# A convolution, a gate and two feed-forward layers on one core: how x reaches its phase layout, and where the context vector is added

## The chip, the cores and the metric

One core of one Trainium2 chip. The metric is the device time of one execution in microseconds (us), the median of the runs. Engines are named as the profile names them: PE (matrix products), PEld (its weight loads), DVE (vector engine), ACT (scalar engine), POOL (GpSimd), SP (the queue that issues most DMAs). A name with a q behind it (SPq, ACTq) is that engine's instruction queue, issuing DMAs.

## What is computed

x has 128 samples of 32 channels by 512 positions, all float32. Only the first layer matters here:

```python
out = conv1d(x, weight, taps=9, pad=4, groups=4)          # per sample, 32 -> 32 channels
ctx = einsum('nd,od->no', cond, c_weight)                  # (128, 32)
h   = out + ctx[:, :, None] + bias[None, :, None]          # a token = (sample, channel), 512 features
logits = h @ W_gate + b_gate                               # 8 experts, top 2 of them
y   = mean over the 2 chosen e of relu(h @ W_e[e] + b_e[e])
x   = x + y
```

There are 4,096 tokens, so 8,192 (token, expert) pairs. The second layer (a per-sample 32 by 32 mix of channels, then one 512 by 512 product with weights unpacked from 4 bits) is the same in both kernels.

## The kernel before

The work runs in three stages. **Stage 1** goes over 32 groups of 4 samples (128 tokens each): it makes the convolution, the gate's logits and the token rows, and scatters each token row to the lists of its two experts in DRAM. **Stage 2** goes over 71 blocks of 128 list entries and multiplies each by its expert's weights. **Stage 3** adds the two results of each token to x and computes the second layer. PE does the stages one after the other; the first block of stage 2 is `product(0, 0)`.

The five engines each run an instruction list of their own, in order, written out by hand as `step1(g, j)` per engine; semaphores carry the dependences. The loop over groups is a hardware loop of four groups a turn for groups 4 to 15, and unrolled elsewhere. What matters in stage 1 is how x becomes the stationary operand of the convolution. A tile `phases` holds, on partition 32*q + i, the positions 4*l + q of input channel i, for l = 0..127 and each of the 4 samples of the group. So three products per sample (`SHIFTS`) make the whole convolution, 12 in a group (L1169).

Per group the kernel before does the following.

- SP loads x of a group, 256 KB, to 128 partitions of `xt`, a ring of four slots (L403), each load when the slot's reader is done. After every four groups it queues a 1 MB load of one expert's weights (`load_we`) and a 257 KB write of zeros (`zero_head`). Once in four groups it also loads 256 KB of `ctx_bc`, the context of those groups' tokens repeated on all partitions (L400), from a copy of it in DRAM (`ctx_d`).
- DVE transposes x in 32 by 32 blocks while it gathers every fourth position (`transpose_x`, L694), two groups ahead. PE transposes four 128 by 128 pieces of that to PSUM (`transpose_phases`, L1098). ACT copies them to `phases` (L567). `phases` and `ring_a` have two slots.
- PE makes the convolution (L1169). DVE adds the context while it evicts (`hT`, L807). PE multiplies each 128 columns of `hT` by the gate's weights beside an identity (L1157, `gate_and_rows`), which gives four partial logits and the token rows; DVE sums the partials (`partial`, L816) and adds `bg_bc` (L825); ACT copies the token rows out, in two copies (`tok`, L584), and two key columns (L574). Then DVE finds the two experts, ending in `chosen` (L854), PE counts ranks with them (L1143, L1144), and POOL scatters (L524).

The order on each engine in step g: PE: convolution of g, transposes for g+1, ranks of g-2, gate of g-1. The gate of g-1 waits for `hT` of g-1, `partial` of g-2 and the `tok` copies of g-2. DVE: `hT` of g, transposition for g+2, then the small instructions for g-1 and g-2. ACT: phase copy for g+1, keys of g-2, token rows of g-1. ACT further issues the loads of the experts' biases in steps 18 to 21, and in steps 24, 25 and 27 does three activations of the second layer's small network (L600, L603, L606), two of them with a table load.

At the end of stage 1 the `xt` slots are reused for lists read back from DRAM: SP's `list_step` loads list a (four DMAs of 64 KB, each to 32 partitions, L434, and one of keys, L437), and for the first four lists waits for `xT_ready` of group 28 + a (L428). DVE transposes list 0 (L921) between its steps 29 and 30, list 1 between 30 and 31 (L943 to L946).

At the start, SP loads the condition and its weights, then the convolution's weights (four small DMAs, L374), then four groups of x. DVE and ACT pick the taps out of them (`pick_taps`, L363), six copies each of 32 by 128 whose reads step 60 bytes; PE transposes them. Eight dummy transposes (`warm_up`) stand ahead of the tap transposes and eight more ahead of the first convolution.

## Time and profile before

| | us |
|---|---|
| median of 3 runs (range) | 514.61 (514.56 to 514.78) |
| the profiled execution's own time | 515.17 |
| its span, first to last instruction | 513.4 |
| stage 1, from the first convolution to the first `product` | 11.6 to 149.7 |
| stage 2, to about | 390 |
| stage 3, to the end | 513 |

| DMA traffic of stage 1, KB a group (from the page's sizes) | |
|---|---|
| x in | 256 |
| expert weights, 1024 KB every fourth group | 256 |
| zeros, 257 KB every fourth group | 64 |
| context, 256 KB every fourth group | 64 |
| scattered rows, 2 times 257 KB | 514 |

Two readings of the page need care. PE's busy share is high in all stages, but they have different limits, so an edit is priced in its own stage. And the modelled length of a matmul overlaps the next one; for PE it is the distance from one start to the next that counts.

### The profile page before, as it was taken

To read this page: it belongs to the slowest core of one execution; us is meant where nothing else is said; L and a number is where in the kernel's file an instruction comes from. 1 tells how busy PE (TensorE), PEld (TensorE's weight loads), DVE (VectorE), ACT (ScalarE), POOL (GpSimd) and SP (SyncE) were. 2 spreads that over 40 slices of the span, in tenths; PEclk is the share of its full clock that TensorE was granted. 3 is DMA by queue.
4 is the path that set the end of the run, shared out by engine and by line. 5 is a ranking of instruction groups with operands and counts; after the bars stand their busy time and mean duration, and the time that the engine had idled before them with its cause. 6 is when DMAs were issued, how large, how long until landed. Compare 5 with 4: busy or idle time off the path is not lost. (4 is left out here: it accounts for less than half of the span.)

```text
span 513.4 us, 10342 instructions
## 1 busy us (share of the span) xinstructions
PE 496.1 (97%) x2412; PEld 329.5 (64%) x2413; DVE 347.0 (68%) x1082; ACT 121.0 (24%) x277; POOL 153.3 (30%) x178
## 2 busy tenths in 40 slices
PE   6999999999999999999999999999997999999996
PEld 5999999999964444444444444444544676767674
DVE  4588888888866547573354445444445899999996
ACT  3232333334421111111111111111123222222220
POOL 9144444444447322233323323332224000000000
PEclk9999999999998999999999999999999999999999
DMA  4969978999885686676665767675554798888852
GB/s 111 290 216 291 274 270 287 324 364 324 235 220 165 200 229 156 166 203 172 176 176 162 184 163 200 163 188 158 150 147 141 252 343 278 288 284 281 296 180 102
DMA packets 91442, 113.07 MB, mean 220 GB/s; under 512 B 25438, under 2 KB 62222, under 8 KB 90372
## 3 DMA queue, kind: packets, MB, share of 16 engines
q1 hardware_dynamic: 73200, 71.26, 49.3%
q0 software_dynamic: 11664, 36.24, 19.3%
q10 hardware_dynamic: 6536, 5.10, 3.5%
q8 instruction: 16, 0.26, 0.2%
q14 instruction: 26, 0.21, 0.1%
HBM read 67.55 MB, written 46.52 MB: 222 GB/s over the span
## 5 line engine op out<-in xcount | busy, mean ns | idle before, releaser
L1196 PE MATMUL bank<-we,lT 128*128 x536 | 233.6, 597 | 1.7 <-DVE ring_a L935 1.6
L1196 PEld LDWEIGHTS bank<-we,lT 128*128 128x128 f32 x536 | 101.7, 191 | 129.0 <-issue 128.8
L935 DVE TENSOR_TENSOR ring_a<-bank,be_bc 128x512 f32<-128x512 f32 x71 | 48.9, 690 | 104.4 <-PE bank L1196 50.4
L541 POOL DMA_INDIRECT pairs_d<-ring_b,pair_i x71 | 71.1, 1002 | 161.3 <-DVE pair_i L924 113.7
L1169 PE MATMUL bank<-wconv,phases 128*128 128x128 f32 x768 | 91.8, 276 | 0.7 <-ACT phases L567 0.7
L620 ACT ACTIVATE ring_b<-ring_a 128x512 f32<-128x512 f32 x71 | 44.7, 631 | 196.7 <-DVE ring_a L935 181.5
L1169 PEld LDWEIGHTS bank<-wconv,phases 128*128 128x128 f32 x768 | 89.1, 193 | 0.9 <-ACT phases L567 0.9
L524 POOL DMA_INDIRECT lists_d<-token_list,row_i x64 | 62.9, 983 | 83.6 <-DVE row_i L845 50.1
L921 DVE STREAM_TRANSPOSE lT<-xt 128x512 f32<-128x512 f32 x71 | 49.8, 702 | 5.7 <-DMA keys<-lists_d 5.4
L1263 PE MATMUL bank<-wq,high 128*128 128x512 f32 x128 | 37.4, 414 | 3.4 <-PEq L1211 3.4
L1157 PE MATMUL bank<-wg,lT 128*128 128x136 f32 x256 | 37.4, 289 | 1.1 <-DVE partial L816 1.1
L694 DVE STREAM_TRANSPOSE ring_a<-xt 128x512 f32<-128x512 f32 x32 | 35.3, 1102 | 0.0
L1267 PE MATMUL bank<-wq,low 128*128 128x512 f32 x128 | 34.5, 391 | 0.0
L567 ACT COPY phases<-bank 128x512 f32<-128x512 f32 x32 | 19.2, 600 | 64.5 <-PE bank L1098 49.2
L807 DVE TENSOR_TENSOR lT<-bank,rows_r 128x512 f32<-128x512 f32 x32 | 22.1, 690 | 16.3 <-PE bank L1169 13.1
L1157 PEld LDWEIGHTS bank<-wg,lT 128*128 128x128 f32 x256 | 31.8, 190 | 1.3 <-issue 1.2
L1242 PE MATMUL bank<-mix_bd,we 128*128 128x128 f32 x224 | 32.2, 287 | 0.0
L1242 PEld LDWEIGHTS bank<-mix_bd,we 128*128 128x128 f32 x224 | 27.3, 191 | 5.7 <-DVE we L1048 5.6
L584 ACT COPY token_list<-bank 128x256 f32<-128x256 f32 x64 | 20.7, 376 | 31.0 <-issue 17.1
L1267 PEld LDWEIGHTS bank<-wq,low 128*128 128x128 f32 x128 | 24.0, 188 | 5.5
L675 ACT CAST high<-bank 128x512 fp32r<-128x512 f32 x32 | 18.7, 586 | 36.3 <-PE bank L1242 36.3
L1263 PEld LDWEIGHTS bank<-wq,high 128*128 128x128 f32 x128 | 21.8, 190 | 7.0 <-issue 4.2
(194 smaller groups left out, 401.4 us busy)
## 6 DMA issues: line engine op xcount, KB each, us to landing
xt<-lists_d SPq DMA_DIRECT2D x284, 64.0 KB
xt<-in_x SPq DMA_DIRECT2D x60, 256.0 KB, 4.1
we<-pairs_d SPq DMA_DIRECT2D x28, 512.0 KB, 4.8
we<-in_L_ffn_W_e SPq DMA_DIRECT2D x8, 1024.0 KB
out<-orow_list SPq DMA_DIRECT2D x32, 256.0 KB, 2.8
lists_d<-orow_list SPq DMA_DIRECT2D x8, 257.0 KB
be_bc<-in_L_ffn_b_e ACTq DMA_DIRECT2D x4, 512.0 KB
words<-pairs_d POOLq DMA_DIRECT2D x4, 512.0 KB, 5.4
```

The source lines that it names most:

```text
L524: pool.indirect_dma_start(lists_d, bass.IndirectOffsetOnAxis(ap=row_i[:, j, k:k + 1], axis=0), token_list[:, j, :], None, bounds_check=E * ...
L541: pool.indirect_dma_start(pairs_d, bass.IndirectOffsetOnAxis(ap=pair_i[:, s % DR:s % DR + 1], axis=0), ring_b[:, s % U, :], None, bounds_c ...
L620: act.activation(ring_b[:, j, :], ring_a[:, j % 2, :], ACT.Relu, scale=0.5).then_inc(result_ready, 1)
L694: dve.transpose(ring_a[:, ja % 2, :].rearrange("m (h q i) -> m q h i", h=MH, q=PH), xt[:, ja, :].rearrange("c (h l q) -> c q h l", h=MH, q ...
L921: dve.transpose(lT[:, ja, :].rearrange("m (p h r) -> m h p r", p=PH, h=MH), xt[:, ja, :].rearrange("r (h p l) -> r h p l", h=MH, p=PH)).th ...
L935: dve.tensor_tensor(ring_a[:, j % 2, :], ps_exp[j % 2][:, :], be_bc[:, bass.ds(expert, 1), :].rearrange("p a n -> p (a n)"), ALU.add).then ...
L1157: mm = pe.matmul(ps_both[:, p // 2, cols], hT[:, ja % 2, p * P:(p + 1) * P], wg[:, p, :], start=True, stop=True)
L1169: mm = pe.matmul(ps_conv[j % 2][:, s * P:(s + 1) * P], phases[:, j % 2, s, t:t + P], wconv[:, t, :, :].rearrange("k p o -> k (p o)"), star ...
L1196: mm = pe.matmul(ps_exp[j % 2][:, :], lT[:, j, p * P:(p + 1) * P], we[:, bass.ds(expert, 1), p, :].rearrange("m a n -> m (a n)"), start=(p ...
L1242: mm = pe.matmul(ps_mix[a % 2][:, q * P:(q + 1) * P], y_of(a)[:, q * P:(q + 1) * P], mix_bd[:, a, :], start=True, stop=True)
L1263: pe.matmul(ps_lin[j][:, :], high[:, j % 2, q * P:(q + 1) * P], wq[:, q, :], start=(q == 0), stop=False, skip_group_check=True)
L1267: mm = pe.matmul(ps_lin[j][:, :], low[:, j % 2, q * P:(q + 1) * P], wq[:, q, :], start=False, stop=(q == PH - 1), skip_group_check=True)
```

## The change

x is loaded so that partition 32*j + c of `xt` (j the ring slot) holds channel c of all four samples, 32 partitions a load (`x_quad`, `x_sub`). `phases` is then filled by four copies of 32 partitions by 512 elements, whose reads step 16 bytes and whose output lies on another quadrant of 32 partitions (`split_phase`): phase 0 by DVE, phases 1 to 3 by ACT. DVE's gathering transposition, PE's four transposes and ACT's copy from PSUM go, with `ps_ph`. Both engines now split two groups ahead, when the convolution of g is done.

The context is no longer added to `hT`. `ctx_col` holds, per partition (sample, channel) and group, context plus `fside`. ACT adds it as a bias in the two row copies (Identity activations), and the logits get it as `gate_bias` = context times the column sums of the gate's weights, plus `b_gate`; both tables are made once, in step 0. The copy of the context in DRAM and its loads go. At the start the first x and the convolution's weights are loaded first, the latter half by SP and half by ACT, and one of the two `warm_up` calls goes. SP's first four list loads now wait for both splits of all 32 groups.

```diff
+        x_sub = x.rearrange("(g s) c l -> g c s l", s=SUB)
         out_g = out.rearrange("(g s) c l -> g (s c) l", s=SUB)
...
         cw_sb = sb("cw_sb", [C, P])
-        cwT = sb("cwT", [P, C])
...
+        def split_phase(copy, q, jq, jb):
+            return copy(phases[q * C:(q + 1) * C, jb, :, 1:P + 1],
+                        x_quad[jq].rearrange("c s (l q) -> c q s l", q=PH)[:, q, :, :])
...
+            sp.dma_start(x_quad[0], x_sub[0]).then_inc(x_in[0], 16)
+            sp.wait_ge(wfull_zero, 1)
+            for s in range(2):
+                rows = slice(s * CG, (s + 1) * CG)
+                sp.dma_start(wfull[rows, rows, PH - 1:PH - 1 + TAPS], conv_w[rows]).then_inc(convw_in, 16)
             sp.dma_start(cond_sb[:, :], cond).then_inc(cond_in, 16)
             sp.dma_start(cw_sb[:, :], ctx_w).then_inc(cond_in, 16)
-            sp.wait_ge(wfull_zero, 1)
-            for s in range(C // CG):
-                rows = slice(s * CG, (s + 1) * CG)
-                sp.dma_start(wfull[rows, rows, PH - 1:PH - 1 + TAPS], conv_w[rows]).then_inc(convw_in, 16)
-            for g in range(XR):
-                sp.dma_start(xt[:, g, :], x_g[g]).then_inc(x_in[g], 16)
-            sp.wait_ge(ctx_ready, 1)
-            sp.dma_start(ctx_d, ctx_sb[:, :]).then_inc(ctx_out, 16)
-            sp.wait_ge(ctx_out, 16)
-            ctx_row = ctx_d.rearrange("(a n) c -> a (n c)", a=1)
-            for i, cols in enumerate((slice(0, CTX_FIRST), slice(CTX_FIRST, CTX_PIECE))):
-                sp.dma_start(ctx_bc[:, cols], ctx_row[:, cols].to_broadcast((P, cols.stop - cols.start))).then_inc(ctx_in[i], 16)
+            for g in range(1, XR):
+                sp.dma_start(x_quad[g], x_sub[g]).then_inc(x_in[g], 16)
+            for s in range(SUB):
+                sp.dma_start(fs_col[s * C:(s + 1) * C, :], fside.rearrange("(c a) -> c a", a=1)).then_inc(fs_in, 16)
...
             with sp.Fori(0, NG // XR - 1) as k:
-                cols = bass.ds(k * CTX_PIECE + CTX_PIECE, CTX_PIECE)
                 for j in range(XR):
-                    if j == 2:
-                        sp.wait_ge(xT_ready, k * XR + 3)
-                        sp.dma_start(ctx_bc[:, cols], ctx_row[:, cols].to_broadcast((P, CTX_PIECE))).then_inc(ctx_in[2], 16)
-                    sp.wait_ge(xT_ready, k * XR + j + 1)
-                    sp.dma_start(xt[:, j, :], x_g[bass.ds(k * XR + XR + j, 1)].rearrange("a p l -> p (a l)")).then_inc(x_in[j], 16)
+                    sp.wait_ge(act_split, k * XR + j + 1)
+                    sp.wait_ge(dve_split, k * XR + j + 1)
+                    sp.dma_start(x_quad[j], x_sub[bass.ds(k * XR + XR + j, 1)].rearrange("a c s l -> c (a s) l")).then_inc(x_in[j], 16)
                 load_we(k + 1)
                 zero_head(k + 1)
...
                     if isinstance(a, int) and a < XR:
-                        sp.wait_ge(xT_ready, NG - XR + a + 1)
+                        sp.wait_ge(act_split, NG)
+                        sp.wait_ge(dve_split, NG)
...
-            act.dma_start(fs_bc[:, :], fside.rearrange("(a c) -> a c", a=1).to_broadcast((P, C))).then_inc(fs_in, 16)
+            act.wait_ge(wfull_zero, 1)
+            for s in range(2, C // CG):
+                rows = slice(s * CG, (s + 1) * CG)
+                act.dma_start(wfull[rows, rows, PH - 1:PH - 1 + TAPS], conv_w[rows]).then_inc(convw_in, 16)
+            act.dma_start(bg_bc[:, :], b_gate.rearrange("(a e) -> a e", a=1).to_broadcast((P, E))).then_inc(bg_in, 16)
             act.wait_ge(ident_ready, 2)
             act.copy(g0[:, 0:1], ident[:, 0:1])
             act.wait_ge(convw_in, 16 * (C // CG))
             pick_taps(act.copy, range(PH // 2, PH), act_taps)
             def step1(g, j):
-                a = g + 1
+                a = g + 2
                 if live(a, NG):
-                    wait(act, ph_done, a + 1)
+                    ja = (j + 2) % U
+                    wait(act, x_in[ja], ring_count(a, ja, XR))
                     wait(act, conv_done, a - 1)
-                    act.copy(phases[:, (j + 1) % 2, :, 1:P + 1].rearrange("k s (h l) -> k h s l", h=MH),
-                             ps_ph[:, :].rearrange("k (h s l) -> k h s l", h=MH, s=SUB)).then_inc(ph_ready, 1)
+                    for q in range(1, PH):
+                        ins = split_phase(act.copy, q, ja, j % 2)
+                    ins.then_inc(act_split, 1)
...
+                    if isinstance(g, int) and a == 0:
+                        act.wait_ge(ctx_ready, SUB)
                     rows = htok[:, ja, :].rearrange("t (h b q l) -> t b q h l", h=MH, b=2, q=2)
                     for b in range(2):
-                        ins = act.copy(rows[:, b, :, :, :],
-                                       ps_both[:, b, 0:2 * (E + P)].rearrange("t (q n) -> t q n", q=2)[:, :, E:].rearrange("t q (h l) -> t q h l", h=MH))
+                        ins = act.activation(rows[:, b, :, :, :],
+                                             ps_both[:, b, 0:2 * (E + P)].rearrange("t (q n) -> t q n", q=2)[:, :, E:].rearrange("t q (h l) -> t q h l", h=MH),
+                                             ACT.Identity, bias=ctx_col[:, bass.ds(a, 1)])
...
-                if isinstance(g, int) and g == -1:
-                    act.dma_start(bg_bc[:, :], b_gate.rearrange("(a e) -> a e", a=1).to_broadcast((P, E))).then_inc(bg_in, 16)
...
-            stepped(act, step1, -1, lo1, hi1, NG + 2)
+            stepped(act, step1, -2, lo1, hi1, NG + 2)
...
-            def transpose_x(a, ja):
+            def split_x(a, ja):
                 wait(dve, x_in[ja], ring_count(a, ja, XR))
-                wait(dve, ph_done, a - 1)
-                dve.transpose(ring_a[:, ja % 2, :].rearrange("m (h q i) -> m q h i", h=MH, q=PH),
-                              xt[:, ja, :].rearrange("c (h l q) -> c q h l", h=MH, q=PH)).then_inc(xT_ready, 1)
+                wait(dve, conv_done, a - 1)
+                split_phase(dve.tensor_copy, 0, ja, ja % 2).then_inc(dve_split, 1)
...
-            transpose_x(0, 0)
+            split_x(0, 0)
             for t in range(SHIFTS):
                 dve.wait_ge(wT_done, t + 1)
                 dve.tensor_copy(wconv[:, t, :, :].rearrange("k p o -> k (p o)"), ps_w[t][:, 0:P]).then_inc(wconv_ready, 1)
+            dve.wait_ge(condT_done, 2)
+            dve.tensor_copy(condT[:, :], ps_misc[:, 0:N]).then_inc(condT_ready, 1)
+            dve.tensor_copy(cwT[:, :, :], ps_misc[:, N:N + C].rearrange("k (a c) -> k a c", a=1).to_broadcast((P, SUB, C))).then_inc(condT_ready, 1)
...
+            def context_columns():
+                dve.wait_ge(ctx_mm, 1)
+                dve.wait_ge(fs_in, 16 * SUB)
+                for s in range(SUB):
+                    rows = slice(s * C, (s + 1) * C)
+                    dve.tensor_scalar(ctx_col[rows, :], ps_misc[rows, 0:N].rearrange("p (g s) -> p s g", s=SUB)[:, s, :],
+                                      fs_col[rows, 0:1], None, ALU.add).then_inc(ctx_ready, 1)
+                dve.wait_ge(gate_sum, 1)
+                dve.wait_ge(ctx_ready, SUB)
+                dve.tensor_tensor(gate_bias[:, :, :], ctx_col[:, :].rearrange("p (g a) -> p g a", a=1).to_broadcast((P, NG, E)),
+                                  bank[0][:, 0:E].rearrange("p (a e) -> p a e", a=1).to_broadcast((P, NG, E)), ALU.mult).then_inc(gbias_ready, 1)
+                dve.wait_ge(gbias_ready, 1)
+                dve.wait_ge(bg_in, 16)
+                dve.tensor_tensor(gate_bias[:, :, :], gate_bias[:, :, :],
+                                  bg_bc[:, :].rearrange("p (a e) -> p a e", a=1).to_broadcast((P, NG, E)), ALU.add).then_inc(gbias_ready, 1)
...
-                if isinstance(g, int) and g in (0, 2):
-                    dve.wait_ge(ctx_in[g // 2], 16)
-                elif j == 0 and live(g, NG):
-                    wait(dve, ctx_in[2], g * (16 // U))
                 if isinstance(g, int) and g >= mlp_first:
                     mix_softmax(g - mlp_first)
                 if live(g, NG):
                     wait(dve, conv_done, g + 1)
                     wait(dve, tok_done, g - 1)
-                    dve.tensor_tensor(hT[:, j % 2, :].rearrange("m (p s o) -> m s p o", p=PH, s=SUB),
-                                      ps_conv[j % 2][:, :].rearrange("m (s p o) -> m s p o", s=SUB, p=PH),
-                                      ctx_bc[:, bass.ds(g * P, P)].rearrange("m (s a o) -> m s a o", s=SUB, a=1).to_broadcast((P, SUB, PH, C)),
-                                      ALU.add).then_inc(hT_ready, 1)
+                    dve.tensor_copy(hT[:, j % 2, :].rearrange("m (p s o) -> m s p o", p=PH, s=SUB),
+                                    ps_conv[j % 2][:, :].rearrange("m (s p o) -> m s p o", s=SUB, p=PH)).then_inc(hT_ready, 1)
+                if isinstance(g, int) and g == 0:
+                    context_columns()
                 if live(g + 2, NG):
-                    transpose_x(g + 2, (j + 2) % U)
...
-                    dve.tensor_tensor(logit[:, :], partial[:, :], bg_bc[:, :], ALU.add).then_inc(logit_ready, 1)
+                    if isinstance(g, int) and a == 0:
+                        dve.wait_ge(gbias_ready, 2)
+                    dve.tensor_tensor(logit[:, :], partial[:, :], gate_bias[:, bass.ds(a, 1), :].rearrange("p a e -> p (a e)"), ALU.add).then_inc(logit_ready, 1)
...
-            def transpose_phases(a, ja):
-                wait(pe, xT_ready, a + 1)
-                wait(pe, ph_ready, a)
-                for h in range(MH):
-                    mm = pe.transpose(ps_ph[:, h * P:(h + 1) * P], ring_a[:, ja % 2, h * P:(h + 1) * P], ident[:, :])
-                mm.then_inc(ph_done, 1)
             pe.wait_ge(ident_ready, 2)
+            warm_up(WARM_START)
             pe.wait_ge(cond_in, 32)
             pe.transpose(ps_misc[:, 0:N], cond_sb[:, :], ident[:, :]).then_inc(condT_done, 1)
             pe.transpose(ps_misc[:, N:N + C], cw_sb[:, :], ident[0:C, 0:C]).then_inc(condT_done, 1)
-            pe.wait_ge(condT_ready, 2)
-            pe.matmul(ps_misc[:, 0:C], condT[:, :], cwT[:, :], start=True, stop=True).then_inc(ctx_mm, 1)
-            warm_up(WARM_START)
...
-            transpose_phases(0, 0)
-            warm_up(WARM_START)
+            def context_products():
+                pe.wait_ge(condT_ready, 2)
+                pe.matmul(ps_misc[:, 0:N], cwT[:, :, :].rearrange("k s c -> k (s c)"), condT[:, :], start=True, stop=True).then_inc(ctx_mm, 1)
+                pe.wait_ge(gate_in, 16)
+                pe.wait_ge(consts, N_CONSTS)
+                for p in range(PH):
+                    mm = pe.matmul(bank[0][:, 0:E], one_row[:, 0:1].to_broadcast((P, P)), wg[:, p, 0:E],
+                                   start=(p == 0), stop=(p == PH - 1))
+                mm.then_inc(gate_sum, 1)
...
-                    wait(pe, ph_ready, g + 1)
+                    wait(pe, act_split, g + 1)
+                    wait(pe, dve_split, g + 1)
...
-                if live(g + 1, NG):
-                    transpose_phases(g + 1, j + 1)
+                if isinstance(g, int) and g == 0:
+                    context_products()
```

## Rows read from the trace of the kernel before

**Rows 1.** The page: busy times over the whole span.
```profile
PE 496.1 (97%) x2412; PEld 329.5 (64%) x2413; DVE 347.0 (68%) x1082; ACT 121.0 (24%) x277; POOL 153.3 (30%) x178
```
**Rows 2.** Timeline of PE, groups 2, 11, 12 and 31 (start, length, line, operation).
```profile
20.36 2.87 PE L1169 MATMUL bank<-wconv,phases 128*128 128x128 f32 x24
...
58.55 2.84 PE L1169 MATMUL bank<-wconv,phases 128*128 128x128 f32 x24
61.23 0.60 PE L1098 MATMUL bank<-ident,ring_a 128*128 128x128 f32 x4
61.67 0.17 PE L1143 MATMUL bank<-chosen,before 128*128 128x8 bf16 x1
...
61.72 1.17 PE L1157 MATMUL bank<-wg,lT 128*128 128x136 f32 x8
62.73 2.84 PE L1169 MATMUL bank<-wconv,phases 128*128 128x128 f32 x24
...
143.37 2.84 PE L1169 MATMUL bank<-wconv,phases 128*128 128x128 f32 x24
```
**Rows 3.** Groups by form of DVE and ACT, whole span (count, busy us, mean ns).
```profile
L694 DVE STREAM_TRANSPOSE ring_a<-xt 128x512 f32<-128x512 f32 x32 | 35.3, 1102 | 0.0
L921 DVE STREAM_TRANSPOSE lT<-xt 128x512 f32<-128x512 f32 x71 | 49.8, 702 | 5.7 <-DMA keys<-lists_d 5.4 <-DVE tab_f L988 0.2
L807 DVE TENSOR_TENSOR lT<-bank,rows_r 128x512 f32<-128x512 f32 x32 | 22.1, 690 | 16.3 <-PE bank L1169 13.1 <-issue 2.7
L620 ACT ACTIVATE ring_b<-ring_a 128x512 f32<-128x512 f32 x71 | 44.7, 631 | 196.7 <-DVE ring_a L935 181.5 <-issue 9.1 <-PE bank L1136 4.1
L584 ACT COPY token_list<-bank 128x256 f32<-128x256 f32 x64 | 20.7, 376 | 31.0 <-issue 17.1 <-DVE partial L816 12.4 <-DMA lists_d<-token_list,row_i 1.5
L668 ACT CAST rows_r<-bank 34x128 fp32r<-34x128 f32 x32 | 8.2, 257 | 46.8 <-PE bank L1249 46.3 <-issue 0.6
L574 ACT COPY token_list<-expert_of 128x2 f32<-128x2 f32 x20 | 3.8, 190 | 5.1 <-DVE expert_of L848 4.5 <-issue 0.6
L363 ACT COPY words<-words 32x128 f32<-32x128 f32 x6 | 2.0, 409 | 3.2 <-DMA words<-in_L_cond_weight 3.2
L603 ACT ACTIVATE g<-bank,b_sb 128x128 f32<-128x128 f32 x1 | 0.4, 384 | 0.0
L600 ACT ACT_TABLE_LOAD x1 | 1.3, 1283 | 0.0
```
**Rows 4.** Timeline, all engines, around the last steps of the group loop.
```profile
129.36 2.08 SPq L434 DMA_DIRECT2D xt<-lists_d  x4
131.48 0.36 SPq L437 DMA_DIRECT2D keys<-lists_d  x1
...
147.60 0.65 ACT L584 COPY token_list<-bank 128x256 f32<-128x256 f32 x2 [1.89 <-DVE partial L816]
148.39 1.17 PE L1157 MATMUL bank<-wg,lT 128*128 128x136 f32 x8 [1.05 <-DVE partial L816]
149.66 3.70 PE L1196 MATMUL bank<-we,lT 128*128 x8
```
**Rows 5.** Timeline of DVE and SP later: a list load that DVE waits for.
```profile
172.77 2.19 SPq L434 DMA_DIRECT2D xt<-lists_d  x4
...
178.38 0.71 DVE L921 STREAM_TRANSPOSE lT<-xt 128x512 f32<-128x512 f32 x1 [1.63 <-DMA keys<-lists_d]
```
**Rows 6.** Stretches of 17 us: busy PE, PEld, DVE, ACT, POOL, clock, DMA share, GB/s.
```profile
84.00:101.00 17.00, 17.00 (x157) 16.95 (x156) 14.46 (x75) 5.33 (x16) 8.50 (x9) 1.00 0.93 291
101.00:118.00 17.00, 17.00 (x157) 16.96 (x157) 14.58 (x79) 5.43 (x17) 8.10 (x9) 1.00 1.01 373
```
**Rows 7.** Timeline of the start.
```profile
1.71 3.02 SPq L374 DMA_DIRECT2D words<-in_L_cond_weight  x4
5.98 1.99 ACT L363 COPY words<-words 32x128 f32<-32x128 f32 x6 [3.24 <-DMA words<-in_L_cond_weight]
11.59 3.50 PE L1169 MATMUL bank<-wconv,phases 128*128 128x128 f32 x24
```

32 lines of the change are left out of this document (12 added, 20 removed).

## The prediction

> **What bounds the kernel now.** I read three views in this order. The page's busy times say that PE works 97% of the span [rows 1]; DVE has 68% and ACT 24%. So time is won only where PE's order of work gets shorter, stage by stage. The timeline of stage 1 shows how: group 11's convolution starts at 58.55, the four transposes for the next group at 61.23, the rank counts at 61.67, the gate at 61.72 and group 12's convolution at 62.73 [rows 2]. PE has no gap in it. The step is 2.68 + 0.44 + 0.05 + 1.01 = 4.18 us. From group 2 to group 31 it is (143.37 - 20.36)/29 = 4.24 us [rows 2]; the 0.06 over the bare step comes a few times per loop turn. The third view, the groups of DVE and ACT by form, gives the prices [rows 3]. ACT does one 0.60 us copy, one key copy and the row pair a step and waits for the rest, so it is the engine with the most room before the change.
>
> **What goes.** PE loses 0.44 us a step: its bare step would be 3.74. DVE loses a 1102 ns transposition [rows 3] and gets one copy of 512 elements. Bounds for that: 1102 if it pays what the gathering transposition pays, and 350 if it were twice as fast as the plain transposition's 702 [rows 3]; I take 0.7, since under 1.1 nothing hangs on it. The eviction of `hT` costs 690 ns with the addition [rows 3], and I give the plain copy the same. DVE's chain of a step then is 0.65 + 0.7 + 1.8 of small instructions = about 3.2 us, under any step below, also with 0.5 more. The loads of `ctx_bc` go, 64 of 1154 KB a group; nobody waited for them.
>
> **What comes on ACT, the term that decides.** Three copies a step whose reads step 16 bytes. No row has such a copy on ACT. Lower end: a contiguous read of 512 elements from SBUF, 631 ns [rows 3]. Upper side: the six tap copies also gather (60 bytes a step) and take 409 ns for 128 elements; a 2-element copy takes 190 [rows 3]. So an element costs (409 - 190)/128 = 1.71 ns, and 512 of them 190 + 876 = 1.07 us. Which one? DVE shows that a step of exactly 16 bytes costs: its transposition with it takes 1102 ns, the same one without it 702 [rows 3], that is 0.78 ns an element more, while 1.71 is 0.84 over ACT's 0.87. I take 1.07. Six back-to-back tap copies take 1.99 us instead of 6 times 0.409 [rows 7], so neighbours overlap by 0.09, and three copies take 3 x 1.07 - 2 x 0.09 = 3.03. The Trainium skill (SBUF — State Buffer, section Door 1: The DMA port swizzle) says that SBUF is read in lines of 16 bytes and that an access which moves to a new line is slower, so that four float32 is as far as one steps for free. By it 16 bytes are no cheaper than 60, which speaks against this layout; it gives no price.
>
> The row pair becomes two activations with a bias per partition. An activation with such a bias takes 384 ns for 128 elements from PSUM, a cast without it 257 [rows 3]; I take 0.11 of the 0.127 as the bias's, so one is 0.49 instead of 0.376 and the pair 0.88 instead of 0.65. ACT's work from the start of its splits to the end of the row pair is then 3.03 + 0.10 (keys, overlapped) + 0.79 = 3.92, near PE's 3.74.
>
> **The new cycle.** The two engines now wait for each other in turn. The row pair ends; 0.14 us later (148.39 - 147.60 - 0.65) the gate's products start [rows 4]; they hold PE for 1.01; the convolution behind them ends 2.84 after its start [rows 2]; only then may ACT split, and its row pair stands behind the splits. That is 0.14 + 1.01 + 2.84 + 0.04 = 4.03 on PE and 3.92 on ACT for two steps. Step = (4.03 + 3.92)/2 = 3.97. I add 0.03 for loop turns, of the 0.06 before: 4.00. Over 29 steps: 29 x (4.24 - 4.00) = **7.0 us gained**, where PE alone promised 12.8.
>
> **ACT's other work, no longer free.** Steps 24, 25 and 27 hold two table loads of 1.28 each and three activations, 0.38 for each of two [rows 3] and about 0.2 for the small one. ACT had idle time there before; now it has under 0.1 us a step. Less the overlaps **3.4 us lost**. The issues of four bias loads lie beside running copies; cost 0, at most 1.3.
>
> **The start.** Before, four weight loads are issued from 1.71 to 4.73, taps begin at 5.98, the first convolution at 11.59 [rows 7]. After, each queue issues two, done near 3.0. ACT then issues one more load (0.3), loads its table (1.28) and copies 0.2: taps from 4.8 to 6.8, splits of group 0 to 9.8. The first convolution took 3.50 against 2.84 later [rows 2, 7], that is below full rate though the dummy transposes ran up to it; without them I take 4.3. Then the context products (a full product and four narrow ones, 1.3, between 0.8 and 2.5) put the second convolution at 15.4, and the third at 15.4 + 2.7 + 1.0 = 19.1, against 20.36 [rows 2]: **1.2 gained**, between 3 and -0.5. DVE's six context instructions (about 1.9) stand ahead of its split of group 2, which still ends before 17.
>
> **The end of stage 1.** SP is moved past the last split. Before, the first list load is issued at 129.36 and its five DMAs take 2.4 to issue [rows 4], long before DVE needs them. After, it waits for ACT's splits of group 31, done 3.1 us after convolution 29 ends. A list that DVE waited for was transposed 178.38 - 172.77 = 5.6 us after its first issue [rows 5]. So list 0 is there at 8.7. DVE has come to it at 3.2 and waits 5.5; behind it stand `hT` 30 and `chosen` of 29, which comes at 8.7 + 0.9 + 3.2 = 12.8. PE wants it after convolution 31, at 2 x 3.97 = 7.9, and stands 4.9. Part of it covers the 1.05 that the gate of 31 waited for DVE anyway [rows 4]: **4.2 lost**, between 2.5 (a load in 4 us) and 6. Lists 1 to 3 follow each other by 2.4 and are in time.
>
> **Sum.** -7.0 + 3.4 - 1.2 + 4.2 = -0.6. Stages 2 and 3 only move. The profiled execution takes 515.17, so 514.6; its like in the runs is 0.56 lower, **514.0**. Most of it hangs on ACT's copy: 0.1 us more or less in each is 0.15 a step, 4.4 us. With 1.0 to 1.15 us for it, and the bounds of start and end, its own range is 509.5 to 518.5.
>
> **Rivals.** *ACT's copy is fast.* If it takes 631 ns, ACT's work is 2.6 and the cycle (4.03 + 2.6)/2 is less than PE's 3.74, which then is the step: 29 x (4.24 - 3.80) = 12.8 gained, ACT's other work is hidden, the splits end sooner, so 1.5 at the start and 3.4 lost at the end: 515.17 - 0.56 - 12.8 - 1.5 + 3.4 = 503.7. For it: only DVE shows a price at 16 bytes. Against: ACT's tap copies. 22%.
>
> *Loads of x into 32 partitions are slow.* This one ends slower. Between 84 and 101 us the DMA engines are busy 93% at 291 GB/s [rows 6], that is 3.9 us of all engines a group. x is 256 of the 1154 KB. If it takes twice the engine time, a group needs 3.9 - 0.2 (context) + 0.9 = 4.6 us, more than any step above, and the rows' scatters, the lists and x come late in turn. It decides from 4.0 us on, a factor of 1.35. With a hard wall the loss is 29 x 0.36 = 10 us; against it stands the stretch from 101 to 118, where 373 GB/s went through at the same pace of PE (157 matmuls in each) [rows 6], so that the wall may lie above. Between, a step of 4.35: 514.6 + 3.2 - 1.2 + 4.2 = 520.8. 11%. No run or row here times a load to 32 partitions alone. The same page of the Trainium skill (its table in that section) has 189 GB/s for partitions 0 to 31 and 328 for all, at 1 MiB; by that the factor is 1.7 and this rival holds.
>
> *The change doesn't relieve PE at all*, since DVE's copy is held up by POOL's scatters by over 0.9 us a step and `chosen` comes late: a step of 4.2, ACT's other work partly hidden, 517.5. 4%.
>
> **How the numbers follow.** The forecast has 63%, spread over -4.5 to +4.5 us: 24% faster, 16% within 0.2% (1.03 us, about what a measurement can tell from none), 23% slower. The fast copy adds 22% to faster, the two slow rivals 15% to slower. Faster 0.46, same 0.16, slower 0.38. The range 502.5 to 519.5 takes in the fast rival's centre with 1 us below it and the forecast's own range; it leaves out some 6% of the fast one and 10% of the slow ones.
>
> **What would show it.** The split copies on ACT near 1.07 us (or 0.63); ACT busy about 95% of stage 1; convolutions 3.97 us apart, in turn shorter and longer; 1.3 to 2.7 us more at steps 24 and 27; DVE idle about 5 us ahead of list 0, ended by the keys' DMA, and PE idle over 4 us ahead of its last rank counts. The prediction is wrong if ACT's copy is off by 0.1 us, if x loads are what the splits wait for, or if PE's first convolution starts after 11.

## The result, and the profile after

The changed kernel is slower: 529.25 us (528.45 to 530.14) beside 514.69 us for the kernel before, a ratio of 1.027 with an interval from 1.024 to 1.030. I had predicted 514.0 us, 502.5 to 519.5, with 0.46 for faster and 0.38 for slower. The time lies above the whole range.

The page of the changed kernel begins with its busy times, as in [rows 1]:

```profile
span 526.7 us, 10141 instructions
## 1 busy us (share of the span) xinstructions
PE 489.2 (93%) x2284; PEld 318.9 (61%) x2285; DVE 340.9 (65%) x1087; ACT 215.1 (41%) x341; POOL 155.6 (30%) x178
```

PE has 7 us less to do and the span is 13.3 us longer than 513.4. The 94 us that ACT gained look harmless as a share of the span, 41%. Stretches of 20 us (columns as in [rows 6]) show where they lie:

```profile
40.00:60.00 20.00, 18.33 (x157) 17.23 (x156) 15.08 (x75) 19.66 (x29) 8.89 (x9) 1.00 0.81 243
...
80.00:100.00 20.00, 17.80 (x156) 17.19 (x155) 15.08 (x78) 19.68 (x29) 9.26 (x10) 1.00 0.82 269
```

ACT, the fourth engine, works 19.66 of 20 us, which is all of it but the gaps between instructions. PE, which had no gap in [rows 6], has 1.7 and 2.2 us of gaps in these stretches. The DMA share is 0.81 where it was 0.93, which speaks against transfers as the limit; `a_flat_read` below tests it. In the groups by form (as [rows 3]) the new work is:

```profile
L367 ACT COPY phases<-xt 32x512 f32<-32x512 f32 x96 | 107.0, 1115 | 3.8 <-PE bank L1182 2.3
L590 ACT ACTIVATE token_list<-bank,ctx_col 128x256 f32<-128x256 f32 x64 | 26.7, 468 | 11.1 <-DVE partial L827 11.1
L818 DVE COPY lT<-bank 128x512 f32<-128x512 f32 x32 | 22.1, 690 | 16.7 <-PE bank L1182 15.8
L367 DVE COPY phases<-xt 32x512 f32<-32x512 f32 x32 | 19.7, 616 | 0.7
```

The same copy takes 1115 ns on ACT and 616 ns on DVE. The third column of ACT's copies, its idle time before them, is 3.8 us for 96 copies: the copies hardly ever waited. The timeline of ACT shows one step whole, from one split to the next:

```profile
59.01 3.36 ACT L367 COPY phases<-xt 32x512 f32<-32x512 f32 x3
62.40 0.19 ACT L578 COPY token_list<-expert_of 128x2 f32 x1
62.49 0.83 ACT L590 ACTIVATE token_list<-bank,ctx_col 128x256 f32<-128x256 f32 x2
63.35 3.40 ACT L367 COPY phases<-xt 32x512 f32<-32x512 f32 x3
```

63.35 - 59.01 = 4.34 us, with no wait in it. Three copies of 1115 ns lie end to end (3.35) without any overlap, although the key copy and the row pair behind them do overlap (62.40 + 0.19 is later than 62.49). The convolutions follow ACT, as the timeline of PE shows:

```profile
20.63 2.84 PE L1182 MATMUL bank<-wconv,phases 128*128 128x128 f32 x24
...
24.35 1.17 PE L1169 MATMUL bank<-wg,lT 128*128 128x136 f32 x8 [0.85 <-ACT token_list L590]
25.35 2.84 PE L1182 MATMUL bank<-wconv,phases 128*128 128x128 f32 x24
```

PE waits ahead of the gate's products for ACT's row pair (L590), which stands behind three split copies. From 22 to 146 us the waits put 11.4 us in 25 waits down to it, and to everything else on PE under 3 us together. From group 2 at 20.63 to group 31 at 150.74 a step takes 130.11/29 = 4.49 us, where [rows 2] gave 4.24. A bare step, one without other work beside it, takes 4.30 to 4.40 us, one like the next: the alternation of shorter and longer steps that I had named as a sign does not appear.

The end of stage 1 in the timeline, to be read beside [rows 4]:

```profile
148.82 1.86 SPq L432 DMA_DIRECT2D xt<-lists_d  x4
...
150.74 2.84 PE L1182 MATMUL bank<-wconv,phases 128*128 128x128 f32 x24
150.87 1.52 SPq L435 DMA_DIRECT2D keys<-lists_d  x1
...
154.91 0.71 DVE L934 STREAM_TRANSPOSE lT<-xt 128x512 f32<-128x512 f32 x1 [6.28 <-DMA keys<-lists_d]
...
156.46 0.84 ACT L590 ACTIVATE token_list<-bank,ctx_col 128x256 f32<-128x256 f32 x2 [6.78 <-DVE partial L827]
...
158.26 0.18 PE L1155 MATMUL bank<-chosen,before 128*128 128x8 bf16 x1 [4.68 <-DVE chosen L867]
158.36 1.64 PE L1169 MATMUL bank<-wg,lT 128*128 128x136 f32 x8
161.25 2.15 PE L1169 MATMUL bank<-wg,lT 128*128 128x136 f32 x8 [1.25 <-ACT token_list L590]
163.19 4.86 PE L1208 MATMUL bank<-we,lT 128*128 x8
```

SP issues the first list load at 148.82, when the last split is done. DVE has the list 6.1 us later and stands 6.28 us for it; PE's last rank counts then wait 4.68 us for `chosen`. Stage 2's first product starts at 163.19, 12.45 us after the last convolution; before it was 149.66 - 143.37 = 6.29 [rows 2, 4].

**Where the 13.3 us lie**, each the difference of a start after and before: the third convolution +0.3 (20.63 against 20.36); the 29 steps to the last +7.1 (130.11 against 123.01); from there to the first product +6.2. That makes +13.5. This product takes 4.86 us instead of 3.70 [rows 4], another 1.2, and what is left up to the end of the span gives 1.4 back.

The last of these has a cause that shows in short stretches (columns as in [rows 6]; PE first, the granted clock behind POOL):

```profile
154.00:158.00 4.00, 0.00 (x0) 0.00 (x0) 2.95 (x18) 1.03 (x3) 0.00 (x0) 1.00 0.39 81
158.00:160.00 2.00, 1.74 (x10) 1.42 (x10) 1.52 (x4) 0.00 (x0) 1.19 (x2) 0.72 0.45 109
160.00:162.00 2.00, 0.75 (x3) 0.79 (x4) 1.82 (x15) 1.03 (x3) 0.77 (x1) 0.50 0.75 214
162.00:164.00 2.00, 2.00 (x8) 1.53 (x7) 1.01 (x4) 0.34 (x1) 1.39 (x2) 0.50 0.75 211
164.00:166.00 2.00, 2.00 (x4) 0.86 (x3) 0.00 (x0) 0.51 (x2) 0.58 (x1) 0.57 0.95 257
166.00:168.00 2.00, 2.00 (x8) 0.78 (x6) 0.00 (x0) 0.00 (x0) 0.00 (x0) 1.00 0.62 151
```

PE does nothing from 154 to 158, waiting for the list. Then its granted clock is 0.50, the level of 1.2 GHz, until about 166. The two gates in it take 1.64 and 2.15 us instead of 1.17, the first expert product 4.86 instead of 3.70: 2.6 us in all, of which 1.5 lie ahead of that product.

### The profile page after: what moved, and what is told of

The parts are those of the page before. It is cut to its first block and busy times, and to the rows that moved or that the text cites. A ratio compares the mean times of both kernels' runs of the same rounds, so it can differ in the third digit from the quotient of the medians.

```text
span 526.7 us, 10141 instructions
## 1 busy us (share of the span) xinstructions
PE 489.2 (93%) x2284; PEld 318.9 (61%) x2285; DVE 340.9 (65%) x1087; ACT 215.1 (41%) x341; POOL 155.6 (30%) x178
## 5 line engine op out<-in xcount | busy, mean ns | idle before, releaser
L367 ACT COPY phases<-xt 32x512 f32<-32x512 f32 x96 | 107.0, 1115 | 3.8 <-PE bank L1182 2.3
L1182 PE MATMUL bank<-wconv,phases 128*128 128x128 f32 x768 | 93.4, 279 | 2.4 <-ACT phases L367 2.4
L522 POOL DMA_INDIRECT lists_d<-token_list,row_i x64 | 64.1, 1001 | 96.6 <-ACT token_list L590 70.0
L1182 PEld LDWEIGHTS bank<-wconv,phases 128*128 128x128 f32 x768 | 90.6, 196 | 2.6 <-ACT phases L367 2.6
L1169 PE MATMUL bank<-wg,lT 128*128 128x136 f32 x256 | 38.7, 296 | 13.8 <-ACT token_list L590 13.1
L1169 PEld LDWEIGHTS bank<-wg,lT 128*128 128x128 f32 x256 | 33.0, 196 | 16.0 <-issue 13.0
L818 DVE COPY lT<-bank 128x512 f32<-128x512 f32 x32 | 22.1, 690 | 16.7 <-PE bank L1182 15.8
L590 ACT ACTIVATE token_list<-bank,ctx_col 128x256 f32<-128x256 f32 x64 | 26.7, 468 | 11.1 <-DVE partial L827 11.1
L672 ACT CAST rows_r<-bank 34x128 fp32r<-34x128 f32 x32 | 8.3, 259 | 47.1 <-PE bank L1261 47.1
```

The lines of the kernel that those rows point to most:

```text
L367: return copy(phases[q * C:(q + 1) * C, jb, :, 1:P + 1], x_quad[jq].rearrange("c s (l q) -> c q s l", q=PH)[:, q, :, :])
L522: pool.indirect_dma_start(lists_d, bass.IndirectOffsetOnAxis(ap=row_i[:, j, k:k + 1], axis=0), token_list[:, j, :], None, bounds_check=E * ...
L1169: mm = pe.matmul(ps_both[:, p // 2, cols], hT[:, ja % 2, p * P:(p + 1) * P], wg[:, p, :], start=True, stop=True)
L1182: mm = pe.matmul(ps_conv[j % 2][:, s * P:(s + 1) * P], phases[:, j % 2, s, t:t + P], wconv[:, t, :, :].rearrange("k p o -> k (p o)"), star ...
```

## The experiments

My theory after this: in steady state the step is ACT's own work and nothing else, and 4.35 - 4.00 comes from the length of the strided copy and the overlap it lacks; the rest is the list wait at the end. The rivals were DMA (x into 32 partitions), DVE's chain, the context's new form, and the long first convolution. The experiments ran in three groups on different chips, and the kernel before took 514.92, 515.40 and 515.82 us beside them. So each ratio below is against the kernel before of its own group, and differences of medians between groups are good to about 1 us.

**Two copies each.** `a_two_two` moves the copy of phase 1 from ACT to DVE.

```diff
-                    for q in range(1, PH):
+                    for q in range(2, PH):
                         ins = split_phase(act.copy, q, ja, j % 2)
...
-                split_phase(dve.tensor_copy, 0, ja, ja % 2).then_inc(dve_split, 1)
+                for q in range(2):
+                    ins = split_phase(dve.tensor_copy, q, ja, ja % 2)
+                ins.then_inc(dve_split, 1)
```

> The changed kernel with phase 1 copied by DVE too, so two copies each. Theory A, ACT's own work is the whole step (three copies of 1.12, keys and rows: 4.36 us, ACT busy without a gap): ACT falls to about 3.25 us a step and no longer bounds; the step becomes PE's 3.8 or DVE's chain (0.65 + 2 x 0.62 + 2.5 = 4.3 at most), so between 3.8 and 4.3 against 4.36 in steps without extras, and ACT's table loads are hidden again. Time 512 to 524. Theory B, the loads of x into 32 partitions or the scatters pace the step: no change, 528 to 530.

Measured: 525.56 us, 1.021 (1.019 to 1.024), above the range of theory A and below that of B. From 40 to 100 us:

```profile
40.00:100.00 60.00, 52.43 (x452) 49.67 (x451) 52.15 (x247) 42.44 (x66) 26.67 (x27) 1.00 0.79 246
```

ACT is down to 42.4 of 60 us, and still the convolutions are 4.39 us apart on average. DVE has taken its place, and the timeline of PE names it:

```profile
60.02 0.18 PE L1157 MATMUL bank<-chosen,before 128*128 128x8 bf16 x1 [0.74 <-DVE chosen L869]
60.12 1.17 PE L1171 MATMUL bank<-wg,lT 128*128 128x136 f32 x8
```

From the start of the `hT` copy (50.63) to the start of the next (55.22) DVE needs 4.6 us, with two copies of 0.6 in it and many short gaps between its small instructions that wait for each other. With one copy that is some 4.0 us, where I had summed 3.2. So taking ACT's excess away is not enough: DVE had 0.35 us of room below 4.35, and the second copy needs more.

**Contiguous reads.** `a_flat_read` has ACT read 512 elements in a row; phases 1 to 3 then hold other positions of x than the convolution needs.

```diff
         def split_phase(copy, q, jq, jb):
+            if q:
+                return copy(phases[q * C:(q + 1) * C, jb, :, 1:P + 1],
+                            x_quad[jq][:, q, :].rearrange("c (s l) -> c s l", s=SUB))
```

> The changed kernel, only ACT's three copies read 512 neighbouring elements instead of every fourth; output and everything else as in the change, so phases 1 to 3 of the convolution get wrong positions of x. Theory A with the 16 byte step as the cause of the price: a copy takes 0.63 us, three of them 1.7 to 1.9, the step is PE's 3.8, the time about 509 (29 x 0.69 less). Rival: the price is that of moving between quadrants of 32 partitions or of DVE and POOL working beside; then the copy stays near 1.1 us and the time at 529.

Measured: 517.78 us, 1.006 (1.004 to 1.009).

```profile
L367 ACT COPY phases<-xt 32x512 f32<-32x512 f32 x96 | 59.1, 616 | 30.6 <-PE bank L1185 29.1 <-issue 0.5
```

Same count, same output tile, same bytes: 616 ns instead of 1115. ACT now waits for PE (30.6 us), a bare step is 3.74 to 3.8 us, PE's own work. The DMA share is 0.91 at 294 GB/s from 40 to 100 us, more than in the changed kernel, with x still going to 32 partitions: the loads keep up with a step of 3.74. The mean step is 3.99, since in the hardware loop some steps take 3.8 to 4.5; there PE's rank counts, which need DVE's `chosen`, start up to 0.55 us late (46.89 - 43.62 = 3.27 us behind their convolution, where 2.72 is usual). The waits name `chosen` for only 1.1 us from 22 to 130, so that DVE holds all of these steps is argued, not shown. The gap to the first product is still 11.8 us (135.94 to 147.72), so this edit leaves the end as it was. These two, the longer mean step and the end, are why the time missed the 509 that I had expected.

**How far apart may the reads be?** `a_step8` lets ACT read every second element, 8 bytes apart; here too the positions are not those that the convolution needs.

```diff
         def split_phase(copy, q, jq, jb):
+            if q:
+                return copy(phases[q * C:(q + 1) * C, jb, :, 1:P + 1],
+                            x_quad[jq][:, :, 0:2 * P].rearrange("c s (l k) -> c s l k", k=2)[:, :, :, q % 2])
```

> The changed kernel, ACT's three copies read every second element (8 bytes a step, two hits in each 16 bytes) instead of every fourth; phases 1 to 3 get wrong positions of x. If the price comes per line of 16 bytes touched, a copy is near the contiguous 0.62 us; if it grows with the step, it lies between, near 0.85; if any step but 4 bytes costs the full price, 1.1.

Measured: 515.27 us in a single execution (the kernel before took 515.82 beside it), and

```profile
L367 ACT COPY phases<-xt 32x512 f32<-32x512 f32 x96 | 62.8, 654 | 28.7 <-PE bank L1185 27.7
```

At 4, 8 and 16 bytes the copy takes 616, 654 and 1115 ns. The price is no slope but a jump between 8 and 16 bytes. With the 190 ns of a tiny copy [rows 3] taken off, an element costs 0.83, 0.91 and 1.81 ns; my tap copies at 60 bytes had given 1.71 [rows 3]. The Trainium skill says as much (Advanced Engine Details and Errata, section Memory Cachelines): SBUF lines have 16 bytes, and two hits on a line are needed to hide the access. At 8 bytes float32 has two hits, at 16 one, and the measured jump agrees. A step of exactly four float32 is thus not free.

**The missing overlap.** In [rows 7] ACT's six tap copies overlapped, in the split they don't. What differs: each split copy writes another quarter of the partitions. `a_same_quad` sends ACT's second and third copy to spare buffers on partitions 32 to 63, those of the first; phases 2 and 3 are missing from the convolution's input.

```diff
         def split_phase(copy, q, jq, jb):
+            if q > 1:
+                return copy((ring_b[C:2 * C, q, :] if jb else ring_a[C:2 * C, q - 2, :]).rearrange("c (s l) -> c s l", s=SUB),
+                            x_quad[jq].rearrange("c s (l q) -> c q s l", q=PH)[:, q, :, :])
```

> The changed kernel, with ACT's second and third split copy writing to other buffers on the partitions of the first (32 to 63), so that the quadrant of the output does not change from copy to copy; phases 2 and 3 of x are then missing from the convolution (zeros). Theory, neighbours do not overlap because the output's quadrant changes: the three copies take 3 x 1.115 - 2 x 0.09 = 3.17 us, the step 4.17, the time some 5 us less than the change, 523. Rival, copies of this kind never overlap: 3.35 to 3.40 as before.

Measured: 524.76 us in a single execution. ACT's timeline:

```profile
60.57 1.13 ACT L370 COPY phases<-xt 32x512 f32<-32x512 f32 x1
61.61 2.13 ACT L367 COPY ring_b<-xt 32x512 f32<-32x512 f32 x2
63.76 0.19 ACT L581 COPY token_list<-expert_of 128x2 f32 x1
63.86 0.83 ACT L593 ACTIVATE token_list<-bank,ctx_col 128x256 f32<-128x256 f32 x2
64.72 1.12 ACT L370 COPY phases<-xt 32x512 f32<-32x512 f32 x1
```

A copy still takes 1.11 us, but the second starts 1.04 us after the first and three last 3.17 us, with 0.09 of overlap at each joint. The step is 64.72 - 60.57 = 4.15 us. The tile changes between the first and the second copy too, and they overlap all the same, so it is not the tile. So 0.2 us of each step is the price of changing the output's partitions from copy to copy. The Trainium skill gives 93 ns of overlap for neighbouring activations (ScalarE: Activation LUTs, section What ACT_TABLE_LOAD costs); the measured 0.09 agrees here, and in the changed kernel it is 0. This run also shows that the step follows ACT's work one to one: 0.2 less in ACT, 0.2 less in the step.

**The end of stage 1.** `a_x_ring` gives x a ring of its own, so that SP's first list loads write into buffers that no split reads and wait for no split. `scale_bc` and `zero_bc` share that ring later.

```diff
-        x_quad = [xt[i * C:(i + 1) * C, :, :] for i in range(XR)]
-        ring_a = sb("ring_a", [P, 2, L])
+        x_ring = sb("x_ring", [P, SUB, L])
+        x_quad = [x_ring[i * C:(i + 1) * C, :, :] for i in range(XR)]
+        ring_a = x_ring[:, 0:2, :]
...
-                    if isinstance(a, int) and a < XR:
-                        sp.wait_ge(act_split, NG)
-                        sp.wait_ge(dve_split, NG)
-                    else:
+                    if not (isinstance(a, int) and a < XR):
```

> The changed kernel with x in a ring of its own (in place of buffers that stage 1 does not use), so that the first four list loads wait for no split. Theory: the 12.45 us from the last convolution to the first product come back to 6.3, PE no longer idles there and its products run at full rate at once, so 6 to 7.5 us less, 522. Rival: the lists come late for another reason (scatters, the early table): less than 2 us gained.

Measured: 521.78 us, 1.013 (1.011 to 1.016), 7.5 us less than the changed kernel. In its timeline DVE transposes a list at 152.96 without a wait, ahead of PE's last rank counts at 153.54:

```profile
150.87 2.84 PE L1179 MATMUL bank<-wconv,phases 128*128 128x128 f32 x24
151.87 0.18 SPq L432 DMA_DIRECT2D keys<-lists_d  x1
152.96 0.70 DVE L931 STREAM_TRANSPOSE lT<-xt 128x512 f32<-128x512 f32 x1
...
157.57 0.69 PE L1205 MATMUL bank<-we,lT 128*128 x1 [0.38 <-issue]
```

6.70 us from the last convolution to the first product, near the 6.29 of before, and this product takes 3.69 us again: by the traces it is done at 161.26 instead of 168.05, 6.8 us earlier. Its last convolution starts at 150.87, the changed kernel's at 150.74: the two losses are independent. `a_two_ring` has both edits.

> Both edits: two copies on each of DVE and ACT, and the ring of its own. If the two causes are separate, the gains add up: the gain of the one plus 6 to 7.5 us, 505 to 518. If DVE's longer chain binds at the end of stage 1, the second gain is smaller than alone.

Measured: 519.44 us, 1.009 (1.006 to 1.011), just above the expected range. The gains don't add up in full: 3.7 for the first edit, 7.5 for the second, 9.8 for both, 1.4 short. The trace shows where. The gap to the first product is 6.74 us, as with the ring alone, but the product takes longer:

```profile
154.60 5.39 PE L1207 MATMUL bank<-we,lT 128*128 x8 [0.42 <-issue]
```

5.39 us instead of 3.69, 1.7 more, and the granted clock is 0.50 from 156 to 158. PE did not stand still for long ahead of it: from 144 us on its longest gap is 1.25 us, as in `a_x_ring`, where the clock stayed at 1.00. So shorter gaps can cost the clock as well; what decides between these two runs is not shown.

**The context alone.** `b_bias` is the kernel before with only the context as a bias: `gate_bias`, the row pair as activations, `hT` as a plain copy, no `ctx_bc`. PE's transpositions stay. Its main lines:

```diff
-                        sp.dma_start(ctx_bc[:, cols], ctx_row[:, cols].to_broadcast((P, CTX_PIECE))).then_inc(ctx_in[2], 16)
...
-                        ins = act.copy(rows[:, b, :, :, :],
+                        ins = act.activation(rows[:, b, :, :, :],
...
-                    dve.tensor_tensor(logit[:, :], partial[:, :], bg_bc[:, :], ALU.add).then_inc(logit_ready, 1)
+                    dve.tensor_tensor(logit[:, :], partial[:, :], gate_bias[:, bass.ds(a, 1), :].rearrange("p a e -> p (a e)"), ALU.add).then_inc(logit_ready, 1)
...
+                if isinstance(g, int) and g == 0:
+                    context_products()
```

> The kernel before with the context part of the change alone: context as bias of the row copies and of the gate, no copy in DRAM, no loads of it; x's way and the order of the start stay. Theory, this part is free and worth nothing since the step is PE's: 514 to 516 (the context products are 1.3 us of PE in step 0). Rival, the longer row pair (0.19 us on ACT) lies in a chain with PE: 29 x 0.19 = 5.5 us more.

Measured: 517.63 us, 1.004 (1.002 to 1.006). The step is (144.43 - 21.21)/29 = 4.25, that of before. The third convolution starts 0.85 us later, at 21.21. Two things stand in front of it: the context products (16.00 to 17.04), and a first convolution of 4.32 us instead of 3.50, whose length differs between executions as told below. The first product starts 1.3 us later, at 150.95. The time is above the 514 to 516 that I expected and below the rival's 5.5 more, which the equal step refutes. So this part costs some 1 to 3 us, at most 1.3 of it in stage 1; where the rest lies I did not trace. It gives nothing back, since DVE's addition and the broadcast loads were hidden.

**The long first convolution.** `a_warm` puts the second group of dummy transposes back ahead of it.

```diff
+            warm_up(WARM_START)
+
             def context_products():
```

> The changed kernel with the eight dummy transposes put back between PE's tap transposes and its first convolution, where PE idles for 2.4 us. Theory, the first convolution takes 5.12 us because PE stood still ahead of it: it goes back to about 3.5, ACT's splits of group 2 start 1.6 earlier, and the whole is 1 to 1.6 us faster than the change, 527.7 to 528.2. Rival, the first convolution is slow whatever stands ahead of it: no change, 529.2.

Measured: 529.64 us, 1.027 (1.024 to 1.030), no change. The first convolution takes 4.85 us instead of 5.12, starts at 11.05 instead of 10.95, and the third starts at 20.45. The eight dummy transposes themselves take 1.97 us, as slow as ever. The granted clock reads 1.00 in every stretch from 8 to 18 us, in this run, in the changed kernel and in the kernel before, whose first convolution took 3.50 [rows 7]. So neither the dummy transposes nor the recorded clock explains the 5.12. The single products show what it consists of. In the changed kernel PE's float32 products of 128x128 take 421 ns in the median from the first dummy at 1.6 us to about 15.5, and 275 ns from there on. In the kernel before they go from 421 to 275 at about 13.0, in `a_no_tables` at about 13.6; there the first convolution takes 4.27 us, though nothing ahead of it was edited. Over the changed kernel and all its variants it takes from 4.27 to 5.46 us (`a_flat_read`). Its length is thus set by its start and by the moment at which the products become shorter, and that differs between executions by more than the 0.27 us of this run. The products of the gate are stretched by nearly the same factor, 434 ns for 279, where the granted clock reads 0.50, at 161 us. Whether the clock is low at the start as well, unrecorded, no run here decides, nor what sets the moment. A gain from the dummies does not show.

**ACT's other work.** `a_no_tables` replaces the small network's Gelu by Relu and its Exp by Square, so that no table is loaded in the group loop; the second layer then mixes with other weights than it should.

```diff
-act.activation(g0[:, :], ps_misc[:, 0:N], ACT.Gelu, bias=b0_sb[:, 0:1])
+act.activation(g0[:, :], ps_misc[:, 0:N], ACT.Relu, bias=b0_sb[:, 0:1])
...
-act.activation(att_x[:, :], att[:, :], ACT.Exp, accum_out=att_s[:, 0:1])
+act.activation(att_x[:, :], att[:, :], ACT.Square, accum_out=att_s[:, 0:1])
```

> The changed kernel with the three activations of the small network in steps 24, 25 and 27 replaced by ones that need no table load (the mix weights of the second layer are then wrong). Theory, ACT has no slack, so its two table loads of 1.28 us stretch stage 1 by their length: 2.4 to 2.6 us less than the change, 526.7. Rival, they hide: 529.2. The two-copy chain can give part back at the end: then 1.3.

Measured: 525.67 us, 1.020 (1.017 to 1.023), 3.6 us less than the changed kernel. The changed kernel had the two loads between its row pair and its split, with no idle time around them:

```profile
123.47 0.83 ACT L590 ACTIVATE token_list<-bank,ctx_col 128x256 f32<-128x256 f32 x2
124.33 1.28 ACT L604 ACT_TABLE_LOAD   x1
125.62 0.37 ACT L604 ACTIVATE g<-bank,b_sb 128x128 f32<-128x128 f32 x1
126.02 3.35 ACT L367 COPY phases<-xt 32x512 f32<-32x512 f32 x3
```

From the convolution of group 24 to that of group 30 the changed kernel takes 146.39 - 116.76 = 29.63 us, this one 142.49 - 115.66 = 26.83, that is 2.8 less for two loads of 1.28. The other 0.9 us lie at the start (third convolution at 19.69 against 20.63). They come from the first convolution, 4.27 us here against 5.12, and are no effect of the tables.

**Room for two copies on DVE.** `a_evict` has two copies each, the ring, and moves the `hT` copy from DVE to ACT, which frees 0.69 us of DVE's chain.

```diff
+                    act.copy(hT[:, j % 2, :].rearrange("m (p s o) -> m s p o", p=PH, s=SUB),
+                             ps_conv[j % 2][:, :].rearrange("m (s p o) -> m s p o", s=SUB, p=PH)).then_inc(hT_ready, 1)
...
-                    dve.tensor_copy(hT[:, j % 2, :].rearrange("m (p s o) -> m s p o", p=PH, s=SUB),
-                                    ps_conv[j % 2][:, :].rearrange("m (s p o) -> m s p o", s=SUB, p=PH)).then_inc(hT_ready, 1)
```

> Two split copies each on DVE and ACT, x in its own ring, and the eviction of the convolution moved from DVE to ACT. Theory, with two copies each DVE's chain (0.65 + 1.24 to 1.4 + 2.65 = 4.6 us in the hardware loop) bounded the step: DVE is left with 3.9 to 4.05, ACT has 0.60 + 2.23 + 0.10 + 0.83 = 3.8, the step falls from 4.40 to 3.95 to 4.1, so 9 to 13 us less than with two copies each and the ring: 507 to 511. Rival, the two engines' turns (eviction, splits and rows in one chain with PE) bind: 4.2 or more, 514 and up.

Measured: 512.32 us, 0.993 (0.990 to 0.995): faster than the kernel before, by less than 1%. It is just above the expected range, as is the step, (140.50 - 19.95)/29 = 4.16. From 40 to 100 us:

```profile
40.00:100.00 60.00, 58.39 (x509) 56.33 (x508) 48.67 (x262) 56.11 (x91) 30.89 (x30) 1.00 0.93 290
```

PE is back at 58.4 of 60 us, now with the shorter list of work, and the DMA share at 0.93, that of before. `a_evict_one` shortens ACT further: the token's row leaves in one activation of 512 elements instead of two of 256, with the gate's partial products 256 columns apart.

```diff
-                cols = slice(p % 2 * (E + P), (p % 2 + 1) * (E + P))
+                cols = slice(p % 2 * 256, p % 2 * 256 + E + P)
...
-                    for b in range(2):
-                        ins = act.activation(rows[:, b, :, :, :],
+                    ins = act.activation(htok[:, ja, :].rearrange("t (h p l) -> t p h l", h=MH, p=PH),
```

> Two copies each, own ring, eviction on ACT, and the token rows copied by one activation of 512 elements instead of two of 256 (the gate's partial products lie 256 columns apart in their two banks). ACT saves 0.83 - 0.70 = 0.13 us a step. If ACT's work alone bounds the step: 29 x 0.13 = 3.8 us less than with two, 508.5; if it is one of two parts of a cycle of two steps: half, 510.4; if DVE bounds: 512.

Measured: 510.22 us, 0.990 (0.986 to 0.993), the fastest of all. One step of ACT:

```profile
59.49 2.26 ACT L367 COPY phases<-x_ring 32x512 f32<-32x512 f32 x2
61.77 0.19 ACT L581 COPY token_list<-expert_of 128x2 f32 x1
61.87 0.68 ACT L591 ACTIVATE token_list<-bank,ctx_col 128x512 f32<-128x512 f32 x1
62.81 0.59 ACT L565 COPY lT<-bank 128x512 f32<-128x512 f32 x1 [0.25 <-PE bank L1179]
63.42 2.25 ACT L367 COPY phases<-x_ring 32x512 f32<-32x512 f32 x2
```

ACT's row takes 0.68 instead of 0.83, and ACT has a wait for PE in each step again. The step is (138.94 - 19.89)/29 = 4.11, the shortest ones 3.74, PE's own work. The first product starts 1.5 us earlier than in `a_evict` (145.49 against 147.00), nearest to the half of 3.8 that I expected of a cycle of two steps; the 2.1 us between the two medians are of different chips and can't tell the three cases apart.

## Why the prediction was wrong, point by point

**What bounds it: right before, wrong after.** PE did lose the transpositions' 0.44 us. I named ACT as the engine that comes near the bound, and it went past it.

**ACT's work of 3.92 us, the step that failed.** I had three copies in 3.03 us. They take 3.37: 0.05 more for each of the three because a copy takes 1115 ns and not 1070, and twice 0.09 because neighbours that write different partitions don't overlap (`a_same_quad`). The overlap was read off six tap copies [rows 7], and I took it over without asking where each copy's output starts. The row pair at 0.83, the key copy at 0.10 and the `hT` copy at 690 ns came out to within 0.05.

**The cycle of 3.97 us.** The mean of PE's 4.03 and ACT's 3.92 holds only as long as neither engine's own work is longer than the mean. With the true 4.35 the mean would be 4.19, but ACT alone needs 4.35, and the step is that. I had noted 4.4 us of loss for each 0.1 us per copy; the true slope past this point is 0.3 us a step, or 8.7 us. So this step failed too: the two engines did not take turns, ACT hardly waited, and the steps were equal. A bare step was 4.35 and not 4.00: 29 x 0.35 = 10.2 us, three quarters of the 13.9 by which the profiled execution (528.45) missed its sum (514.6). The first step adds 0.4.

**ACT's other work, 3.4 us: right.** The six steps from 116.76 to 146.39 take 29.63 us where six bare ones take 26.1, 3.5 us more, and `a_no_tables` takes 2.8 of it away with the two loads. But the kernel before was not bare there either: its same six steps take 139.20 - 113.13 = 26.07 us, 1.0 more than six of 4.18. I had put the 0.06 over its bare step down to loop turns; over half of it lies in these six steps. Against the kernel before, ACT's other work cost 2.5 us.

**The start, -1.2: wrong by 1.5, though within its bound of -0.5.** ACT's last issue ended at 4.15, its table load at 5.47, and the taps began at 5.58 and not at 4.8; the first convolution started at 10.95 instead of 9.8 and took 5.12 instead of 4.3. The second convolution started 5.99 us after the first, where I had 5.6. `a_warm` shows that missing dummy transposes were not the reason for the length; since it differs by over 1 us between executions, no better figure for it could have been given.

**The end, +4.2: right in kind, 6.2 in size.** The order of waits was as told: keys, DVE, `chosen`, rank counts. PE stood 4.68 us there (4.9 predicted). The step that failed is that I counted PE's stand as its length alone. The half clock behind it adds 1.5 us ahead of the first product and 1.2 within it. Nor was part of the stand covered, as I had it: the gate of 31 still waited 1.25 us, now behind ACT's row pair. In `a_x_ring` PE never stands longer than 1.25 us, the granted clock stays at 1.00 from 154 to 168, and nearly all of it comes back: 6.8 us by the traces, 7.5 between the medians. My bound was 6.

**The rivals.** The fast copy is refuted by 1115 ns, and its price was also too good: `a_flat_read` has the copy at 616 and yet a mean step of 3.99, not 3.80, where DVE's chain, longer in the hardware loop than I summed, is the likely limit. The slow loads of x are refuted: they landed in 3.8 us (median, issue to landing) against 4.1 before, with the DMA share falling to 0.81, and `a_flat_read` ran steps of 3.74 with them. The Trainium skill's table (SBUF — State Buffer, section Door 1: The DMA port swizzle) has less than 60% of the rate for 32 partitions; nothing of it showed at 256 KB a group among these other transfers. The third, DVE held so that PE isn't relieved, did not happen in the steps: DVE's copy took 616 ns, less than my 0.7. Beside ACT's slow copies DVE decides only once it has two itself (`a_two_two`).

**The chances.** My own range for the forecast ended at 518.5. It held ACT's copy between 1.0 and 1.15, and 1.115 lies inside; what it did not hold was the steeper slope beyond the cycle's mean, and that start, step and end could all fall on the slow side. Of the three things that I said would show the prediction wrong none happened: the copy was off by 0.045 us, the splits did not wait for loads of x, and the first convolution started at 10.95. They all watched the inputs of the sum, and what failed was the rule that made a step out of them, and the clock.

## What to carry to other kernels

Add up each engine's own work per step in the stage that counts, not over the span: ACT had 41% of the span and 98% of stage 1, and whoever hands work from a full engine to an idle one must compare that sum with the full one's new step. A copy that reads float32 16 bytes apart takes 1.8 times a contiguous one on ACT here: give ACT few of them, or find a layout with two elements a line. If a buffer is reused in the next stage, look at who waits for its last reader: a ring of its own was worth about 7 us, as much as the shorter steps were meant to give.
